# A two-layer kernel on one Trainium2 core: the first layer's experts computed for the two chosen per token only

## The reference, cut to what matters

```python
logits = ...                                  # (2048, 8), from q, k, v of 8 each
top_logits, idx = top_k(logits, 2)
scores = softmax(top_logits)
for e in range(8):                            # w1[e]: (704, 128), w2[e]: (128, 352)
    a, g = split(x_rep @ w1[e].T)             # 352 + 352
    he = (silu(a) * g) @ w2[e].T
    out += where(expert_ids == e, he, 0)
combined = (out * scores).reshape(2048, 2, 128).sum(axis=1)
```

## Time and profile before

| | us |
|---|---|
| median of 3 runs | 523.91 (523.36 to 526.57) |
| profiled execution, its time | 524.22 |
| profiled execution, its span | 522.40 |
| PE busy | 442.2 (85%) |
| DVE busy | 382.8 (73%) |
| ACT busy | 278.1 (53%) |
| POOL busy | 194.8 (37%) |

### The profile page before, as it was taken

The page is one execution under the profiler, slowest core; times in us unless marked ns, Lnnn a source line. Parts: engine busy times, 40 slices in busy tenths (PEclk is TensorE's granted clock), DMA queues, the critical chain, the costliest instruction groups (busy, mean ns, idle before and its releaser), DMA issues.

```text
span 522.4 us, 7319 instructions
## 1 busy us (share of the span) xinstructions
PE 442.2 (85%) x2143; PEld 325.9 (62%) x2143; DVE 382.8 (73%) x702; ACT 278.1 (53%) x392; POOL 194.8 (37%) x188
## 2 busy tenths in 40 slices
PE   2729999999999999999989969299689778977893
PEld 1327887888878888788877845155455445544452
DVE  5687478944888448894498987776768877887784
ACT  2375674426644275533655255835676577557730
POOL 1248014400144001530002100740477778777850
PEclk9958999999999999999999979579799999999997
DMA  6420001100012000000000000000265776687664
GB/s 177 96 61 23 2 0 43 43 1 0 0 41 52 0 0 0 0 0 0 1 0 2 1 0 1 0 2 0 55 130 114 144 141 131 116 157 137 126 130 120
DMA packets 29535, 26.76 MB, mean 51 GB/s; under 512 B 10837, under 2 KB 25414, under 8 KB 29510
## 3 DMA queue, kind: packets, MB, share of 16 engines
q0 software_dynamic: 4608, 16.78, 16.8%
q1 hardware_dynamic: 24902, 9.69, 7.3%
HBM read 8.64 MB, written 1.05 MB: 19 GB/s over the span
## 4 chain that ended last, share of the span: by engine, by line
PE 29%; DVE 28%; POOL 19%; issue 13%; ACT 7%; DMA 2%; DVEq 1%; SPq 0%; POOLq 0%; ACTq 0%
POOL state L435 9%; PE psum L1083 7%; PE psum L203 6%; PE psum L205 6%; PE psum L204 6%; POOL xn_tok L439 4%; POOL g_hi L448 3%; DVE hid L771 2%; PE psum L1203 2%; DVE at_m L800 1%; DVE at_m L802 1%; POOL g_lo L449 1%; DVE xn_tok L693 1%; POOL sel_now L450 1%; PE psum L1218 1%
## 5 line engine op out<-in xcount | busy, mean ns | idle before, releaser
L567 ACT ACTIVATE sil<-psum 128x512 f32<-128x512 f32 (+1 forms) x96 | 56.3, 596 | 104.3 <-PE psum L205 91.2
L771 DVE TENSOR_TENSOR hid<-sil,psum 128x512 f32<-128x512 f32 (+1 forms) x96 | 65.1, 686 | 51.8 <-PE psum L205 32.9
L1083 PEld LDWEIGHTS psum<-e_w,hid 128*128 128x128 f32 (+1 forms) x768 | 94.9, 191 | 6.0
L1083 PE MATMUL psum<-e_w,hid 128*128 128x128 f32 (+1 forms) x768 | 95.3, 274 | 0.0
L203 PE MATMUL psum<-xn_hi,e_hi 128*128 128x512 f32 (+1 forms) x192 | 81.8, 426 | 7.9 <-DVE hid L771 7.3
L975 DVE TENSOR_TENSOR_SCAN state<-dec,win_t 128x1024 f32<-128x1024 f32 x32 | 73.4, 2295 | 20.0 <-ACT dec L643 20.0
L205 PE MATMUL psum<-xn_lo,e_hi 128*128 128x512 f32 (+1 forms) x192 | 76.0, 396 | 0.0
L204 PE MATMUL psum<-xn_hi,e_lo 128*128 128x512 f32 (+1 forms) x192 | 75.8, 395 | 0.0
L652 ACT ACTIVATE sil<-psum,vec_t 128x512 f32<-128x512 f32 x64 | 43.2, 687 | 47.3 <-PE psum L205 36.8
L435 POOL TENSOR_SCALAR state<-state,ssm_cb 128x1024 f32<-128x1024 f32 x32 | 49.7, 1552 | 45.2 <-DVE state L975 42.2
L1258 PE MATMUL psum<-hid,g_w 128*128 128x512 f32 x128 | 61.3, 592 | 0.0
(11 more groups left out here) (261 smaller groups left out, 766.5 us busy)
## 6 DMA issues: line engine op xcount, KB each, us to landing
xn_tok<-state POOLq DMA_DIRECT2D x32, 512.0 KB, 4.5
e_raw<-in_L_ffn_w SPq DMA_DIRECT2D x16, 128.0 KB, 2.1
e_raw<-in_L_ffn_w SPq DMA_DIRECT2D x8, 176.0 KB, 2.4
res<-in_L_attn_x SPq DMA_DIRECT2D x4, 256.0 KB, 3.9
g_raw<-in_L_ffn_w SPq DMA_DIRECT2D x16, 64.0 KB, 2.3
g_w<-in_L_ffn_w SPq DMA_DIRECT2D x16, 64.0 KB, 2.5
out<-res SPq DMA_DIRECT2D x4, 256.0 KB, 2.9
e_raw<-in_L_ffn_w SPq DMA_DIRECT2D x16, 48.0 KB, 1.9
```

The lines of the kernel that those rows point to most:

```text
L567: act.activation(sil[0:M, s % 2, :], ps[s % 2][0:M, :], ACT.Silu).then_inc(silu_done, 1)
L771: dve.tensor_tensor(hid[0:M, tb % 2, ft, :], sil[0:M, s % 2, :], ps[2 + s % 2][0:M, :], ALU.mult).then_inc(gated, 1)
L1083: ins = pe.matmul(ps[4 + o % 2][:, n * P:(n + 1) * P], hid[0:m, tb % 2, ft, n * P:(n + 1) * P], e_w2[j][0:m, ft, :], start=(ft == 0), stop ...
```

## The change

The dense loop over experts goes. All eight experts are turned, copied and split in the opening (`turn_expert`, `copy_expert`, POOL's loop over `E0`) into `w_hi`, `w_lo` (128 x 8 x 704) and `w_out` (128 x 8 x 384). Each token's two assignments get slots in an array in DRAM, `slots`, grouped by expert, each expert's group padded to whole tiles of 128: `NTILE` = 2048 x 2 / 128 + 7 = 39 tiles, always all computed. The slot numbers come from two matmuls (`lower`, `ones` by `chosen`) and a chain of small DVE instructions. POOL scatters the rows (128 features, the weight, the number of the destination row) with 32 indirect DMAs of 128 rows of 520 bytes. SP loads one tile after another into a ring of six (`x_tile`). Per tile: PE turns it, ACT copies the high part, DVE subtracts for the low part; PE makes a and g with the tokens as the stationary and the weights as the moving operand (6 matmuls of 352 columns, the expert chosen by a number that PE reads from SBUF with `value_load`); ACT silu, DVE gate; PE turns the result (3 transposes), ACT copies it, PE multiplies by w2 (3 matmuls of 128 columns, after a second `value_load`), ACT weighs and copies, and POOL scatters the 128 result rows into `parts` in DRAM by an indirect DMA. At the end SP loads `parts` back as `both` (2 MB), and DVE adds it to `res`.

The attention's steps stand in one list of 4 x 25. The first 33 are done ahead of the first tile; the other 67 are spread over the 39 tiles, one or two to a tile (`beside`). PSUM: one bank each for a, g, the turned input, the turned hidden and the output; banks 6 and 7 for the attention. `Fori` is gone from this part. All statistics between the layers are taken after the last `both` has landed.

```diff
+    NTILE = NTOK * TOPK // P + E0 - 1
+    XRING, ORING = 6, 3
+        AHEAD_STEPS = 33
@@ SP
+            for e in range(2, E0):
+                sp.wait_ge(e_turned, 2 * (e - 2) + 2)
+                load_expert(e, e % 2)
+            sp.wait_ge(fill_ready, 1)
+            sp.dma_start(slots.rearrange("(n p) r -> p n r", p=P),
+                         fill[:, None, :].to_broadcast([P, NTILE, ROW])).then_inc(slots_filled, 16)
...
+            sp.wait_ge(scattered, 16 * NT * TOPK)
+            for n in range(NTILE):
+                if n >= XRING:
+                    sp.wait_ge(o_sent[(n - XRING) % ORING], 16 * ((n - XRING) // ORING + 1))
+                sp.dma_start(x_tile[n % XRING][:, :], slots[n * P:(n + 1) * P, :]).then_inc(x_tile_in[n % XRING], 16)
@@ POOL
+            for e in range(E0):
+                pool.wait_ge(e_copied, 2 * e + 1)
+                split(e_t[e % 2][:, :], w_hi[:, e, :], w_lo[:, e, :])
...
+            pool.wait_ge(slots_ready, 1)
+            pool.wait_ge(slots_filled, 16)
+            for t in range(NT):
+                for k in range(TOPK):
+                    pool.indirect_dma_start(
+                        out=slots, out_offset=bass.IndirectOffsetOnAxis(ap=to_slot[k][:, t:t + 1], axis=0),
+                        in_=rows[k][:, t, :], in_offset=None).then_inc(scattered, 16)
             own(pool.memset(sel[:, :], 0.0))
...
+            def send(n):
+                pool.wait_ge(o_out, n + 1)
+                pool.wait_ge(part_ready, n + 1)
+                pool.indirect_dma_start(
+                    out=parts, out_offset=bass.IndirectOffsetOnAxis(ap=part[:, n:n + 1], axis=0),
+                    in_=t_out[n % ORING][:, :], in_offset=None).then_inc(o_sent[n % ORING], 16)
@@ ACT, one tile
+            for n in range(-2, NTILE + 2):
+                if 0 <= n < NTILE:
+                    tile_silu(n)
+                if n + 2 < NTILE:
+                    copy_x(n + 2)
+                if 0 <= n - 1 < NTILE:
+                    copy_hidden(n - 1)
+                if n >= 2:
+                    weigh_out(n - 2)
+                if 0 <= n < NTILE:
+                    for i, s in beside(n):
+                        attention(i, s)
@@ DVE
+            own(dve.tensor_copy(place[:, :, :], total))
+            own(dve.tensor_tensor_scan(flat(upto), ones[:, 0:P], flat(place), 0.0, ALU.mult, ALU.add))
...
+            dve.nop().then_inc(slots_ready, 1)
...
+            for n in range(-2, NTILE):
+                if 0 <= n < NTILE:
+                    gate(n)
+                if n + 2 < NTILE:
+                    split_x(n + 2)
+                if 0 <= n < NTILE:
+                    for i, s in beside(n):
+                        attention(i, s)
@@ PE
+            def hidden(n):
+                e = expert_of(n)
+                pe.wait_ge(x_lo_ready, n + 1)
+                if n >= 1:
+                    pe.wait_ge(gated, n)
...
+            for n in range(-2, NTILE + 2):
+                if 0 <= n < NTILE:
+                    hidden(n)
+                if n + 2 < NTILE:
+                    turn_x(n + 2)
+                if 0 <= n - 1 < NTILE:
+                    turn_hidden(n - 1)
+                if n >= 2:
+                    output(n - 2)
+                if 0 <= n < NTILE:
+                    for i, s in beside(n):
+                        attention(i, s)
```

More of the change, by code:

```diff
@@ L146, in program @@
[L146 to L153, removed]
+        fill = sb("fill", [P, ROW])
+        numbers = sb("numbers", [P, NTILE], mybir.dt.int32)
+        spare = sb("spare", [P, NTILE])
+        part = sb("part", [P, NTILE], mybir.dt.uint32)
@@ L154, in program @@
+        state = [later(f"state_{k}", [P, NTOK // 2]) for k in range(4)]
+        hid = later("hid", [P, 2, NF, TB])
+        sil = later("sil", [P, 2, TB])
+        base = here()
         dt_t = sb("dt_t", [P, NTOK])
@@ L157, in program @@
         cw_hl = sb("cw_hl", [P, NTOK], F32R)
+        first = over(base, nc.sbuf_base)
+        rows = [first(f"rows_{k}", [P, NT, ROW]) for k in range(TOPK)]
+        x_tile = [first(f"x_tile_{r}", [P, ROW]) for r in range(XRING)]
+        proj_hi = first("proj_hi", [P, 6, P], F32R)
+        proj_lo = first("proj_lo", [P, 6, P], F32R)
+        wo_sb = first("wo_sb", [P, P])
+        lower = first("lower", [P, P])
+        upto = first("upto", [P, E0, NT])
+        place = first("place", [P, E0, NT])
+        u_t = xr_tok[:].rearrange("p a b -> p (a b)")
+        y_t = xn_tok[:].rearrange("p a b -> p (a b)")
         sel_now = [sb(f"sel_now_{j}", [P, P], F32R) for j in range(2)]
@@ L365, in _, with attend, attention @@
                 split_group(j)
[L367 to L376 removed]
+            def attend(out, a, b, op):
+                pool.tensor_tensor(out, a, b, op).then_inc(att_pool, 1)
+            def attention(i, s):
@@ L774, in turn, with flat @@
-            def turn(i, last):
-                att = Chain(dve, att_dve, i * N_ATT_DVE + 1)
+            dve.wait_ge(ranked, 1)
+            before, total = (ps[0][:, n * P:(n + 1) * P].rearrange("p (t e) -> p e t", e=E0) for n in range(2))
+            n_e, tiles, upto_tiles, shift, prior = (per_e[:, n, :] for n in range(5))
+            last, whole, second, unused = (per_t[:, n, :] for n in range(4))
+            def flat(a):
+                return a[:, :, :].rearrange("p e t -> p (e t)")
+            own(dve.tensor_copy(place[:, :, :], total))
@@ L874, in turn @@
-                if not last:
-                    gate(i + 1, 0)
-                attention(STEPS)
-                if not last:
-                    gate(i + 1, 1)
-                add_output(OUTS - 1)
-                assert att.n == N_ATT_DVE
-            for s in range(2):
-                gate(0, s)
-            with dve.Fori(0, NB - 1) as i:
-                turn(i, False)
-            turn(NB - 1, True)
-            dve.wait_ge(o_added, NB * OUTS + 2)
+                if s == 2:
+                    pe_step(1)
+                    act_step(1)
+                    att(dve.tensor_tensor(A["kv"], ps[7][:, :], A["k"], ALU.mult))
```

691 lines of the change are left out of this document (368 added, 323 removed).

## The result

The changed kernel takes 556.8 us (median of 4 runs, 555.39 to 557.45) against 523.93 for the kernel before, measured beside it: a ratio of 1.0616, with an interval of 1.058 to 1.0652. The profiled execution has 557.0 us and a span of 555.3. The forecast of 532 had the sign right and the size wrong: 33 us were lost, not 8. It lies outside the forecast's own range (515 to 548) and inside the wide one (486 to 575).

The account below looks back on a forecast made before the run. PE's dense products bound the old kernel; in the changed loop the ring was expected to. Opening 138, loop 156, border 18.5, second layer 217.5 and 1.8 around the span gave 531.8, forecast 532 us; own range 515 to 548, wide 486 to 575.

Parts of the forecast that it names:

- the ring: In the loop, reloading one of six x slots waits for an earlier tile's scatter: 3.7 us a tile, the expected bound.
- the chain's 2.3: In a tile, hidden, silu, gate and hand-overs follow one another through the single banks: 2.3 us.
- B: The loop over 39 tiles at 4.0 us each: 156 us, 95 less than 250.9.
- lumps: Attention work falls unevenly beside the tiles; the 1.4 us between ring and chain swallow most, 0.3 us a tile added.
- 26: Opening's serial end, from two POOL attention operations through batch 0, batch 1's sixth projection and first tiles: 26 us.
- 60.5: In the opening, DVE's slot chain of 7.5 us ends and the scatters can start at 60.5 us.
- The first rival: Scatters cost POOL 0.65 us and land in 2.3, so the change pays: 490 us in all, chance 0.37.
- The second rival: PE's clock falls in the loop, making a tile 4.5 us: 552 us in all, chance 0.16.
- The third rival: Indirect DMAs cost POOL 2.1 us each, lengthening opening and loop: 576 us in all, chance 0.13.
- C: Border between loop and second layer: emptying, last scatter, loading results back, additions and statistics; 18.5 us, 10 more than 8.4.
- s: In the loop, a result scatter's time from issue to landing: taken as 3.0 us, between 2.3 and 4.5.
- v: In the loop, PE's reading of the expert number: taken as 0.5 us, between nothing and 1.28.

Follow-up runs that it names:

- Experiments 3 and 7: Changed kernel with POOL's layer-two work behind the attention's POOL operations: 544.44 us; then also batch 0's four POOL attention operations among the scatters: 527.45 us.
- experiment 2: Changed kernel with all attention steps ahead of the first tile, none beside the tiles: 636.56 us.
- experiment 6: Changed kernel with all attention ahead of the tiles and x slots freed at the weighing, not at the scatter's landing: 614.83 us.
- experiment 9: Changed kernel with 200 unread products of 512 columns in PE's idle stretch of the opening: 559.64 us.
- both edits of the loop: Each alone on the changed kernel: x slots freed at the weighing, 550.34 us; two banks for a, with a made first, 549.9 us.
- experiment 8: Changed kernel with x slots freed at the weighing, two banks for a, layer-two work behind attention, four attention operations among the scatters: 515.55 us.
- experiment 11: The kernel of experiment 8 with ranking ahead of expert 5 and the filling of slots behind expert 3's load: 516.28 us.

## Why the prediction was wrong

**What held.** That PE would cease to bound; that the six prepared experts, the slot chain, the 32 scatters, layer two's work and the rest of batch 0 would be one serial path through POOL. 32 scatters at 1.31 are 41.9 (1.2 and 38.4 in the sum), layer two's part 12.7 (12.9), the slot chain 7.0 (7.5). Experiments 3 and 7 are direct proof: moving 12.7 us of POOL's work off this path brought the first tile 13.8 forward, and moving four operations between the scatters another 12.3 (135.93 to 123.64). The direction of the whole came from this. DVE's and ACT's loads were right too: 88.00 / 38 = 2.3 and 92.73 / 38 = 2.4 us a tile, as forecast. Neither of the two signs that were to prove the prediction wrong came: a scatter costs 1.27 to 1.31 (0.8 to 1.5 were allowed) and a tile 4.23 (3.5 to 4.5). It failed by parts that are all too small, and the largest share is the opening's.

**The step that failed in the loop (9 us): "It is the bound I expect", of the ring, and "The 1.4 us by which ring and chain differ swallow most; I add 0.3".** The ring sets the time of a tile only where no attention stands beside the tiles, and there it was 3.40 and not 3.7 (experiment 2), since the load lands after 1.9 and the scatter after 2.23 where I took 2.3 and 3.0. The estimate of 2.15 by the Trainium skill (DMA: Bandwidth & Descriptors, Anatomy of one DMA) was the nearer one. The bare tile without the ring takes 2.78, not the chain's 2.3: PE alone has 2.5 us of work in it. So ring and chain differ by 0.62 and not by 1.4, and of the attention far less is swallowed: it adds 0.83 to the ring (3.40 to 4.23), not 0.3, and 1.31 where the scatter is out of it (2.78 to 4.09). Seen from the other side, the ring is worth 0.62 in the bare loop and 0.14 beside the attention. The two hide each other in part, by 0.48.

I had compared averages (2.25 for DVE, 2.4 for ACT) with the longest round and let the shorter hide in the longer. But silu and gate are in the same in-order queues as the attention and on the chain that frees the single banks: silu starts 0.54 later and the gate 0.63 later in a mean tile than in the bare loop (table in experiment 6), and a tile with little attention beside it gains nothing back (the shortest take 2.63, a bare one 2.78). The observation that I had named as the refutation, PE waiting for `gate` instead of `x_tile`, is what the trace shows. That B was only 9 under is partly luck: a ring 0.3 too long stood against lumps 0.5 too short.

**The step that failed in the opening (11.7 us): the serial end, "26", and the start of the scatters, "60.5".** The end was 31.3 (118.4 to 149.7). The rest of batch 0 behind POOL's two operations took 16.4, near the 15.3 of the sum. What I had too short was the stretch of batch 1 to its sixth projection: 10.1 (137.34 to 147.42) for my 5. In it is the cold clock, which I had at nothing there: by the distances some 3 us on the 15 projection products of 139.03 to 146.69 (0.43 against 0.23), and 1 on the eight small ones (2.04, and 1.06 at the full clock in experiment 9's loop). This is an estimate; where experiment 9 gave nine of the fifteen the full clock back, the first tile came 0.7 earlier and not 1.8. ACT's table load of 1.28 was missing from the sum too. The scatters began at 63.65, held by the slot chain until 62.27 and by the filling, which landed at 62.74 (POOL's own row names it as releaser); the 32 cost 3.5 more. Layer two's work is as forecast.

**The first rival, 490.** Its ring was near (3.4 against 3.40) and its landing too (2.3 against 2.23). It did not come, because a scatter costs POOL 1.27 and not 0.65, and because the lumps don't hide.

**The second rival, the clock.** The loop averages 0.88, above the 0.75 from which I let it decide. What the lower level costs in the loop is at most some 7 us by the estimate in experiment 9, or 0.18 a tile; the opening shows it too (above).

**The third rival.** Scatters cost 1.27 back to back, under the 1.5 at which I let them decide.

**C's 3.** "two take 9.5" supposed that the load of 2 MB sets the end, with 3.5 of DVE behind the last block. In the chain the first block lands 3.83 after its issue, and then DVE needs 10.7 for four blocks, 0.9 more until the normalisation. Emptying took 3.7 and not 2.5 (from the end of the 39th tile's slot, 314.67, to the last scatter at 318.40), and the scatter 2.23 and not 3.0. The sum was closer than its parts.

**Slips in the sums.** The ring's lower end, with s at 2.3 and v at nothing, is 3.1 and not 3.2, and the first rival's ring is 3.4 and not 3.35. Neither moves the forecast.

**What stays open.** C, which no experiment varied; the clock's exact share in the loop; and whether the loop gets shorter when the attention's operations stand elsewhere in the queues, or with more buffers: only one bank for a was added.

## What to carry to other kernels

When work is taken off the engine that bounds a loop, list for each other engine the whole in-order queue of an iteration, with the foreign operations and table loads that stand ahead of the one on which a buffer depends: most of their length adds to the iteration (here 0.83 us to a round trip of 3.40, or 1.31 to one of 2.78), and does not hide in its longest round trip. A second bank for a, with a made first, took back 0.13; whether deeper buffers would cover the lumps was not tried. Price the new opening as a serial path through the engine that issues its DMAs, and look what else is parked in that queue: here the order of POOL's instructions (experiments 3 and 7, 29 us) was worth more than both edits of the loop (13 us), and together they turned a loss of 6.2% into a gain of 1.8%.

## What was not expected of the hardware

- An indirect DMA of 128 rows holds POOL 0.97 us, back to back, with a gap of 0.30 to the next. Next to attention work it showed up to 1.97 (experiment 8).
- Four of the 23 small operations of DVE's slot chain, of 8 and of 128 columns, took 1.5 to 1.8 us in place of 0.2 to 0.4 when they started beside one of POOL's splits of 1.68, and ended within 0.3 us of its end (experiment 11). In the changed kernel itself POOL was done with its splits at 52.9 and the chain was clean. The Trainium skill tells of a port that the two lock against each other (SBUF — State Buffer, Who interferes with whom); these rows agree, and the price falls on short operations.
- The filling of 2.5 MB took 17.1 us to land, and the DMA behind it in SP's queue took 8.85 us to issue in experiment 11 and 9.11 in the changed kernel, where the loads of the experts show 0.43.
- The landing of a scatter varies: mostly 2.2, but single ones up to 4.7 (the changed kernel). Such a one can hold a tile up (experiment 9).
- After 13.35 us of idleness PE's clock had fallen although 46.9 us of dense products lay before (experiment 9).
